# Seven PSUM banks given out by a plan of what is free first, and three small operations on the attention maxima moved

## The chip, the cores and the metric

The program runs on one core of one Trainium2 chip. The metric is the device time of one execution, in microseconds (us); lower is better. TensorE is called PE here (its weight loads PEld), VectorE is DVE, ScalarE is ACT, GpSimd is POOL, and SP is the engine that issues most DMAs.

## What is computed

The input is a batch of 4 sequences of 1024 tokens of width 128. Two transformer layers follow each other, each with 16 heads of width 8 and with attention and feed-forward side by side on the same normalised input:

```
xn = layernorm(x);  x = x + attention0(xn) + experts(xn)      # rotary, full softmax; top 2 of 8 experts, 128 -> 512 -> 128
xn = layernorm(x);  x = x + attention1(xn) + gated_fp4(xn)    # causal softmax; 4-bit rounded weights and activations, 128 -> 352 -> 128
```

Everything is fp32. The softmax is exact: each row's own maximum is subtracted before the exponential.

## The kernel before

**One order, written by a planner.** The class `Plan` (line 43) lays out 491 slots on the host, before the kernel is built. Every engine then walks the same list of slots and issues its own share of each, in order. The eight (layer, sequence) pairs are eight phases; a phase of layer 0 has 64 steps, one of layer 1 has 48, together 448.

**A slot.** A step of attention is one group of four heads against 128 keys and 512 queries. In its slot the function `products` makes, for each of four heads j, a matmul E (keys by queries, 50 rows contracted, 512 columns, in bf16) into one PSUM bank. ACT takes its exponential into `PR` (line 854), and PE multiplies that by the values into the bank `pO` in the slot after (eight fp32 matmuls). Beside each E stands a matmul M of scores the other way round (queries by keys, 48 rows) for a step twelve slots later (`AHEAD`). DVE takes the row maxima of M (line 1201, or line 1205 with the causal mask added) into `mparts`. E and M of the same j use different row halves of PE and are issued as a pair; PE waits for the banks of both before it issues either. So a slot takes eight banks for E and M.

**The maxima.** When a quarter of a phase's heads has its maxima for 512 queries ("combine", 64 times), DVE reduces `mparts` to the negated maximum `mneg` (128 x 16, line 1437), copies it to bf16 as its high part (line 1439), and writes the rest as the low part (line 1440), both into `msplit`. One slot later the event "mtr" turns `msplit` with one small matmul into a bank of the ring; DVE copies it to `mT` in bf16 (line 1473), and SP writes `mT` with four DMAs into two rows of `QX` (line 659). With these rows E comes out of the matmul with the maximum already subtracted.

**Everything else** ("xs", 551 events with the "mtr" ones) is spread by `Plan` over the slots: projections, transposes, the experts' tiles ("unit" and "y"), the fp4 feed-forward ("gu", "turn", "down"), and the ends of attention ("fin", "of", "fp"). PE does a slot's events after the second pair of products. Each event fills one bank, and either ACT or DVE empties it, as `ON_VECTOR` says. DVE's small steps (statistics, routing, scales) are planned into quarters of slots.

**The banks.** PSUM has eight banks: `pO`, and a ring of seven (`RING`). `number` (line 285) writes all 4135 fillings (E, M and events) in the order in which PE makes them, and filling number r uses bank r mod 7:

```
    def bank(self, kind, k):
        return self.at[kind][k] % RING
...
                def vacant(kind, k):
                    r = plan.at[kind][k] - RING
                    if r >= 0:
                        was, of = plan.ring[r]
```

so that PE always waits (in `vacant`) for the filling seven places back: on `s_ex` (an E read by ACT), `s_mr` (an M read by DVE) or `s_freed` (an event's bank).

Of the kernel before, what the change touches and what calls it, by code (L numbers as in the profile page):

```python
# [7 lines left out]
P = 128  # L8
HALF = 512
TH = HALF // P  # L10
DK = 8
G = 4
# [3 lines left out]
E, FC = 8, 4  # L16
# [3 lines left out]
PHASES = [(0, 0), (0, 1), (1, 0), (0, 2), (1, 1), (0, 3), (1, 2), (1, 3)]  # L20
# [7 lines left out]
RING = 7  # L28
# [4 lines left out]

ON_VECTOR = ("pj", "lg", "rt", "mtr", "fin", "gu", "down", "fp")
HEAVY = {"unit": 24, "y": 6, "turn": 11, "xT": 10, "v": 11, "cT": 10, "xqT": 10, "of": 10, "wT": 10,
         "pj": 11, "mtr": 8, "fin": 15, "gu": 8, "down": 5, "fp": 11, "lg": 5, "rt": 5}
SMALL = {"stats": 9, "means": 10, "norm": 12, "best": 5, "which": 8, "hits": 7, "comb": 12, "rem": 11, "wq": 15,
         "xq": 9, "hq": 6}  # L40


class Plan:
# [8 lines left out]
    def __init__(self):  # L52
        self.slots = []
        self.start = []
        self.place = {}
        at = LEAD + AHEAD
        for layer, b in PHASES:
            self.start.append(at)
            at += len(STEPS[layer])
        self.end = at  # L60
        for p, (layer, b) in enumerate(PHASES):
            i = self.start[p]
            for s in STEPS[layer]:
                self.slot(i)["step"] = (p,) + s
                self.slot(i + 1)["pv"] = (p,) + s
                g, qh, kt = s
                if g % 2 and kt == self.kts(p, qh) - 1:
                    self.slot(i + 1)["out"] = (p, g // 2, qh)
                    self.force(i + 2, ("fin", p, g // 2, qh))
                i += 1  # L70
            i = self.start[p] - AHEAD
            for q in QUADS[layer]:
                self.slot(i)["quad"] = (p,) + q
                g, qt, kh = q
                if qt % TH == TH - 1 and kh == (NH - 1 if layer == 0 else qt // TH):
                    self.slot(i)["combine"] = (p, g, qt // TH)
                    self.force(i + 1, ("mtr", p, g, qt // TH))
                    self.slot(i + 2)["sp"].append(("rows", p, g, qt // TH))
                i += 1
        self.prepare(0, 0)  # L80
        self.weights(12)
        for b in range(2):
            self.slot(LEAD + AHEAD - 2 + 24 * b)["sp"].append(("zero", b))
        for p, (layer, b) in enumerate(PHASES):
            if layer == 0:
                self.finish(p)
                if p:
                    self.tiles(p)
            else:
                self.finish(p)  # L90
            if p + 1 < len(PHASES):
                if PHASES[p + 1][0] == 0:
                    self.prepare(p + 1, self.start[p] - 20 if p else self.gated[p] + 2 * T + 2)
                    if p == 0:
                        self.tiles(p)
                else:
                    lead = max(self.start[p], self.done[PHASE_OF[0, PHASES[p + 1][1]]]) + 1
                    self.prepare(p + 1, lead)
        self.number()

    def kts(self, p, qh):
        return T if PHASES[p][0] == 0 else TH * (qh + 1)
# [44 lines left out]
    done = {}  # L147
# [137 lines left out]
    def number(self):  # L285
# [6 lines left out]
        for s in self.slots:  # L292
# [34 lines left out]
            for e in s["pool"]:  # L327
                if e[0] == "round" and e[-1] == POOL_STEPS - 2:
                    self.pools[e[1:-1]] = len(self.pools)

    def bank(self, kind, k):
        return self.at[kind][k] % RING


PLAN = Plan()
# [2 lines left out]
def two_layer_block(nc, x, wqa0, wqb0, wka0, wkb0, wv0, wo0, gate_w, gate_b, w1, b1, w2, b2wo,  # L338
# [3 lines left out]
    ALU, ACT, X = mybir.AluOpType, mybir.ActivationFunctionType, mybir.AxisListType.X  # L342
    plan = PLAN

    B, S, D = x.shape
# [19 lines left out]
    with ctx:  # L365
# [39 lines left out]
        stats = sb("stats", [P, T, 6])  # L405
# [13 lines left out]
        mparts = [sb(f"mparts{i}", [P, NH, G * TH, NH]) for i in range(2)]  # L419
        mneg = sb("mneg", [P, G * TH])  # L420
        msplit = sb("msplit", [P, 2 * G * TH], bf16)
        mT = sb("mT", [2 * G * TH, P], bf16)
# [22 lines left out]
        at = [sb(f"at{i}", [P, 2 * T], u32) for i in range(2)]  # L445
# [4 lines left out]
        cT = sb("cT", [E + 1, HALF])  # L450
# [5 lines left out]
        hq = sb("hq", [P, F1])  # L456
# [4 lines left out]
        xqT = sb("xqT", [P, S])  # L461
# [10 lines left out]
        s_x, s_freed = sem("s_x"), {"A": sem("s_xA"), "D": sem("s_xD")}  # L472
        s_pv, s_oT = sem("s_pv"), sem("s_oT")
        s_ng, s_row = sem("s_ng"), sem("s_row")
# [26 lines left out]
        xs = [nc.dram_tensor(f"rows_in{i}", (NT * P, D), f32, kind="Internal").ap() for i in range(2)]  # L501
# [19 lines left out]
        for o, w in ((0, wg), (o_up, wu)):  # L521
            for c in range(FC1):
                n = min(P, F1 - P * c)
# [23 lines left out]
        def copy(dst, src):  # L547
            return nc.scalar.activation(dst, src, ACT.Copy)  # L548
# [13 lines left out]
        def filled(e):  # L562
            return plan.xs[e] + 1
# [23 lines left out]
        with nc.Block() as block:  # L587
# [250 lines left out]
            def _(act):  # L838
# [19 lines left out]
                for i, s in enumerate(plan.slots):  # L858
# [5 lines left out]
                    if s["out"] is not None:  # L864
                        k = plan.outs[s["out"]]
# [7 lines left out]
                    for e in s["act"]:  # L873
                        _, p, q, h = e
                        n = plan.parts[p, q, h]
                        half = slice(HALF * h, HALF * h + HALF)
# [9 lines left out]
                    for e in s["xs"]:  # L886
                        if plan.by[e][0] == "A" or (e[0] == "gu" and e[3] == 0) or (e[0] == "pj" and e[4] == ""):
                            act.wait_ge(s_x, filled(e))
                        src = bank(e)
                        if e[0] == "xT":  # L890
                            _, p, h = e
                            layer, b = PHASES[p]
                            copy(flip[:, HALF * h:HALF * h + HALF], src[:, :]).then_inc(s_freed["A"], 1)
                        if e[0] == "pj" and e[4] == "":
                            _, p, q, h, _ = e
# [15 lines left out]
                        if e[0] == "y":  # L911
                            N, n = tile(*e[1:]), e[2]
                            if N >= 2 and n >= 0:
                                act.wait_ge(s_ys[N % 2], 16 * (N // 2))
                            c = slice(D if n < 0 else 0, D if n == NT - 1 else D + P)
                            copy(yx[N % 2][:, c], src[:, c]).then_inc(s_freed["A"], 1)
                        if e[0] == "unit":
# [6 lines left out]
                            for fc in range(FC):  # L924
                                ins = nc.scalar.activation(hid[N % 2][:, P * fc:P * fc + P], src[:, P * fc:P * fc + P],  # L925
                                                           ACT.Relu, bias=b1r[N % 2][:, fc:fc + 1])
# [3 lines left out]
                        if e[0] == "gu":  # L930
                            _, p, t, up = e
                            b = PHASES[p][1]
                            if up:
                                continue
                            if t or b:

                                was = (p, t - 1) if t else (PHASE_OF[1, b - 1], T - 1)
                                act.wait_ge(*freed(("gu",) + was + (0,)))
                            nc.scalar.activation(th[:, :], src[:, 0:F1], ACT.Tanh, scale=0.5).then_inc(s_th, 1)
                        if e[0] == "turn":  # L940
                            copy(hqT[:, 0:FC1 - 1, :], src[:, 0:(FC1 - 1) * P])
                            copy(hqT[0:FL, FC1 - 1, :], src[0:FL, (FC1 - 1) * P:FC1 * P]).then_inc(s_freed["A"], 1)
                        if e[0] == "of":
                            copy(ofT[:, :], src[:, :]).then_inc(s_freed["A"], 1)
                        if e[0] == "wT":
# [5 lines left out]
                    for e in s["late"]:  # L951
                        if e[0] == "mid":
                            _, p, q, h = e
                            n = plan.parts[p, q, h]
# [5 lines left out]
                        if e[0] == "abs":  # L960
                            n = plan.pools[e[1:]]
                            width = quantized(e[1:])[2]
# [4 lines left out]
            def _(pe):  # L967
                pe.wait_ge(s_wA, 16 * len(loads_a))

                def vacant(kind, k):  # L970

                    r = plan.at[kind][k] - RING
                    if r >= 0:
                        was, of = plan.ring[r]
                        if was == "E":
                            pe.wait_ge(s_ex, of + 1)
                        if was == "M":
                            pe.wait_ge(s_mr, of + 1)
                        if was == "X":
                            pe.wait_ge(*freed(of))  # L980
# [41 lines left out]
                for s in plan.slots:  # L1022
                    products(s, 0)
                    if s["pv"] is not None:
                        p, g, qh, kt = s["pv"]
                        n = plan.steps[s["pv"]]
# [8 lines left out]
                        first = kt == 0 and g % 2 == 0  # L1035
# [9 lines left out]
                    for e in s["xs"]:  # L1045
                        vacant("X", plan.xs[e])
                        dst = bank(e)
                        if e[0] == "xT":
                            _, p, h = e
                            for t in range(TH):  # L1050
                                pe.wait_ge(s_xn, T * p + TH * h + t + 1)
                                ins = turn(dst[:, P * t:P * t + P], xn[PHASES[p][0]][:, TH * h + t, :])
                        if e[0] == "pj":
                            _, p, q, h, part = e
                            layer, b = PHASES[p]
# [3 lines left out]
                            src = flip  # L1059
# [108 lines left out]
            def _(dve):  # L1168
# [9 lines left out]
                def count(ins):  # L1178
                    nonlocal counted
                    counted += 1  # L1180
                    ins.then_inc(s_dve, 1)

                def link(ins):
                    count(ins)
                    own()
# [243 lines left out]
                for s in plan.slots:  # L1429
# [4 lines left out]
                    if s["combine"] is not None:  # L1434
                        layer = PHASES[s["combine"][0]][0]
                        dve.wait_ge(s_mr, 4 * (plan.quads[s["quad"]] + 1))
                        link(v.tensor_reduce(mneg[:, :], mparts[layer][:, s["combine"][2], :, :], axis=X, op=ALU.max,
                                             negate=True))
                        link(v.tensor_copy(msplit[:, 0:G * TH], mneg[:, :]))
                        v.tensor_tensor(msplit[:, G * TH:2 * G * TH], mneg[:, :], msplit[:, 0:G * TH],  # L1440
                                        ALU.subtract).then_inc(s_ng, 1)
                    for e in s["small"][2]:
                        small_step(e)
                    for e in s["xs"]:
# [21 lines left out]
                                                  ALU.add)  # L1466
                        if e[0] == "rt":
                            ins = v.tensor_copy(before[:, :], src[:, 0:E * 2 * T + E])
                        if e[0] == "mtr":
                            k = plan.mtrs[e[1:]]  # L1470
                            if k:
                                dve.wait_ge(s_row, 64 * k)
                            ins = v.tensor_copy(mT[:, :], src[0:2 * G * TH, 0:P])
                        if e[0] == "fin":
                            _, p, g, qh = e
                            o4 = src[:, :].rearrange("p (q j w) -> p q j w", j=G, w=OW)
# [82 lines left out]
```

## Time and profile before

| | |
|---|---|
| median of 3 runs | 1598.43 us (1593.64 to 1598.57) |
| the profiled execution | 1606.22 us, of which its span is 1604.5 us |
| granted clock of PE, mean | 0.956 |
| instructions in the span | 34217 |

The profile gives one execution: busy time of each engine, what it waited for and who released it, the chain of work that ended last (followed back from the end to what released each piece), and each instruction's start. The median is used for the prediction; its steps are worked out on the profiled execution, whose own time is 7.8 us above that median.

### The profile page before, as it was taken

The numbers are of one execution on the slowest core, as the hardware profiler recorded it, in microseconds if no ns is written. First come the engines' busy times: TensorE is split into PE (matmuls) and PEld (weight loads), VectorE is DVE, ScalarE is ACT, GpSimd is POOL, SyncE is SP. The second block draws the span as 40 slices with busy tenths as digits, with TensorE's granted clock in tenths as the row PEclk, the third lists the DMA queues.
The fourth block names the chain that finished last, engine by engine and source line by source line (L and its number), as shares of the span: only waits on it lengthen the run. The fifth ranks groups of instructions, "written<-read, shape, count | busy, mean of one in ns | idle before, by whom it ended". The sixth has DMA issues, their size and how long they took to land.

```text
span 1604.5 us, 34217 instructions
## 1 busy us (share of the span) xinstructions
PE 1459.2 (91%) x10557; PEld 583.9 (36%) x10557; DVE 1338.2 (83%) x3450; ACT 1129.7 (70%) x2580; POOL 578.4 (36%) x531
## 2 busy tenths in 40 slices
PE   3978989999999899989999999989999988989986
PEld 1112344443333544432333444333433432323332
DVE  6999877789887698999888789889878779978991
ACT  2267678788787467777878767768878845765675
POOL 3002302103253456440242263660152464554443
PEclk8599999999999899999999999999999977989998
DMA  6403273333271452221451135123372100600000
GB/s 172 102 8 100 73 184 110 106 87 91 88 183 52 120 116 83 59 82 36 134 120 51 37 113 134 49 82 99 111 165 82 39 26 2 152 9 15 2 2 14
DMA packets 169833, 131.84 MB, mean 82 GB/s; under 512 B 31597, under 2 KB 143158, under 8 KB 169654
## 3 DMA queue, kind: packets, MB, share of 16 engines
q1 hardware_dynamic: 165562, 121.26, 28.5%
q0 software_dynamic: 4096, 8.40, 1.7%
q8 instruction: 91, 1.49, 0.4%
q14 instruction: 84, 0.69, 0.1%
HBM read 88.50 MB, written 40.50 MB: 80 GB/s over the span
## 4 chain that ended last, share of the span: by engine, by line
PE 58%; DVE 26%; issue 6%; ACT 5%; POOL 3%; DMA 1%; SPq 0%; another core or an unknown queue 0%; DVEq 0%; ACTq 0%; POOLq 0%
PE ring L542 38%; PE pO L542 17%; DVE mparts L1201 15%; PE ring L545 3%; ACT PR L854 3%; DVE junk L1205 2%; DVE xr L1381 1%; DVE stats L1251 1%; ACT hid L925 1%; DVE hs L1493 1%; DVE xr L1501 1%; DVE am L1414 1%; DMA b1r<-in_b 1%; ACT parts L548 0%; DVE hs L1489 0%
## 5 line engine op out<-in xcount | busy, mean ns | idle before, releaser
L854 ACT ACTIVATE PR<-ring 128x512 f32<-128x512 f32 (+3 forms) x1792 | 882.4, 557 | 344.8 <-PE ring L542 333.7
L1201 DVE TENSOR_REDUCE mparts<-ring 128x1 f32<-128x512 f32 x1280 | 808.5, 682 | 84.4 <-PE ring L542 77.1
L542 PE MATMUL ring<-QX,KX 50*128 50x512 bf16 (+3 forms) x1792 | 543.7, 366 | 77.2 <-DVE mparts L1201 35.5
L542 PE MATMUL ring<-KX,QX 48*128 48x512 bf16 (+3 forms) x1792 | 556.8, 374 | 14.2 <-DMA QX<-scratch 14.1
L542 PE MATMUL pO<-PR,VX 128*18 128x512 f32 (+3 forms) x3584 | 444.0, 568 | 6.5 <-ACT PR L854 5.2
L542 PEld LDWEIGHTS ring<-QX,KX 50*128 50x128 bf16 x1792 | 127.5, 94 | 609.0 <-ACT PR L854 220.3
L1205 DVE CUSTOM_DVE_ANT_0 junk<-ring,diag 128x384 bf16<-128x384 f32 (+3 forms) x512 | 228.8, 486 | 46.0 <-PE ring L542 41.2
L811 POOL TENSOR_SCALAR bq<-bq 128x352 f32<-128x352 f32 (+1 forms) x40 | 47.2, 1179 | 349.7 <-ACT bq L964 349.3
L784 POOL DMA_INDIRECT rows_in<-xn,at x64 | 63.7, 996 | 228.8 <-PE pO L542 144.8
L542 PEld LDWEIGHTS ring<-KX,QX 48*128 48x128 bf16 x1792 | 127.3, 94 | 33.6 <-DVE mparts L1201 17.9
L925 ACT ACTIVATE hid<-ring,b1r 128x128 f32<-128x128 f32 x368 | 105.0, 369 | 27.7 <-PE ring L542 26.2
L542 PE MATMUL ring<-yx,w1r 128*128 128x128 f32 x736 | 107.8, 291 | 7.7 <-DMA b1r<-in_b 4.8
L542 PEld LDWEIGHTS pO<-PR,VX 128*18 128x18 f32 x3584 | 60.6, 96 | 132.0 <-issue 88.0
L800 POOL DMA_INDIRECT ra<-rows_out,at x64 | 61.6, 963 | 125.4 <-PE pO L542 89.2
L542 PEld LDWEIGHTS ring<-yx,w1r 128*128 128x128 f32 x736 | 91.7, 196 | 34.3 <-DVE mparts L1201 23.3
L542 PE MATMUL ring<-w2r,hid 128*128 128x128 f32 x736 | 97.5, 275 | 0.0
L542 PEld LDWEIGHTS ring<-w2r,hid 128*128 128x128 f32 x736 | 93.2, 197 | 0.9 <-issue 0.5
L767 POOL TENSOR_TENSOR parts<-rb,parts 128x512 bf16<-128x512 f32 x30 | 35.0, 1166 | 115.3 <-ACT parts L548 115.3
L542 PE MATMUL ring<-identb,laterb 128*128 128x128 bf16 x512 | 75.2, 230 | 0.0
L825 POOL TENSOR_SCALAR yq<-yq 128x352 f32<-128x352 f32 (+1 forms) x40 | 60.3, 1508 | 3.3
L820 POOL TENSOR_TENSOR bq<-hq,bq 128x352 f32<-128x352 f32 x64 | 59.7, 933 | 4.6
L548 ACT ACTIVATE yx<-ring 128x256 f32<-128x256 f32 (+1 forms) x96 | 36.0, 375 | 35.2 <-PE ring L542 33.8
(165 smaller groups left out, 1349.8 us busy)
## 6 DMA issues: line engine op xcount, KB each, us to landing
w1r<-in_w SPq DMA_DIRECT2D x92, 256.0 KB
w2r<-in_w SPq DMA_DIRECT2D x92, 256.0 KB
scratch<-parts SPq DMA_DIRECT2D x48, 256.0 KB, 3.3
scratch<-parts SPq DMA_DIRECT2D x96, 128.0 KB, 2.3
KX<-scratch SPq DMA_DIRECT2D x64, 192.0 KB, 4.4
QX<-scratch SPq DMA_DIRECT2D x128, 96.0 KB, 5.0
xg<-rows_in SPq DMA_DIRECT2D x92, 64.0 KB
rows_out<-yx SPq DMA_DIRECT2D x92, 64.0 KB
```

Of the source, the lines that this page charges most:

```text
L542: return nc.tensor.matmul(dst, lhsT, rhs, start=start, stop=stop, **kw)
L545: return nc.tensor.transpose(dst, src, ident[0:src.shape[0], 0:src.shape[0]])
L548: return nc.scalar.activation(dst, src, ACT.Copy)
L784: nc.gpsimd.indirect_dma_start(xs[b % 2], bass.IndirectOffsetOnAxis(at[b % 2][:, c:c + 1], 0), xn[0][:, c % T, :], None).then_inc(s_sc[b], 16)
L800: nc.gpsimd.indirect_dma_start(yg[:, D * t:D * t + D], None, ys[b % 2], bass.IndirectOffsetOnAxis(at[b % 2][:, c:c + 1], 0)).then_inc(s_yg ...
L811: ins = nc.gpsimd.tensor_scalar(b_, b_, 1.0, None, ALU.max)
L820: ins = nc.gpsimd.tensor_tensor(b_, dst, b_, ALU.subtract)
L825: ins = nc.gpsimd.tensor_scalar(y, y, SHIFT, SHIFT, ALU.add, ALU.subtract)
L854: nc.scalar.activation(PR[:, n % 2, HALF * j + off:HALF * j + HALF], ring[plan.bank("E", k)][:, off:HALF], ACT.Exp, scale=SCALE).then_inc( ...
L925: ins = nc.scalar.activation(hid[N % 2][:, P * fc:P * fc + P], src[:, P * fc:P * fc + P], ACT.Relu, bias=b1r[N % 2][:, fc:fc + 1])
L1201: v.tensor_reduce(dst, src[:, 0:w], axis=X, op=ALU.max).then_inc(s_mr, 1)
L1205: v.tensor_tensor_reduce(out=junk[k % 2][:, 0:w], in0=src[:, 0:w], in1=diag[:, HALF - w:HALF], scale=1.0, scalar=NEG, op0=ALU.add, op1=ALU ...
```

## The change

Three things are changed. `banks`, a new function of `Plan`, walks the slots with a list of work for PE, ACT and DVE, with constant costs for each piece and a constant lag between engines, and gives each filling the bank that by these costs is free first; it remembers whose bank that was (`was`), and `vacant` waits for that filling. The number of banks, PE's order and each engine's order of the events stay. Second, the copy of the turned maxima to `mT` goes from DVE to ACT, where it is done among the slot's events, after the slot's exponentials. Third, the high part of the maxima is no longer a copy of `mneg`, but a second reduction straight from `mparts` with bf16 output, which does not wait for the first. Because DVE no longer copies `mT`, the combine now waits in so many words for the "mtr" matmul before it (`s_x`).

```
-ON_VECTOR = ("pj", "lg", "rt", "mtr", "fin", "gu", "down", "fp")
+ON_VECTOR = ("pj", "lg", "rt", "fin", "gu", "down", "fp")
...
+ON_TENSOR = {"unit": 13, "y": 14, "turn": 8, "xT": 11, "v": 13, "cT": 11, "xqT": 11, "of": 11, "wT": 10, "pj": 17,
+             "mtr": 4.6, "fin": 11, "gu": 12.5, "down": 9, "fp": 18, "lg": 13, "rt": 8}
+
+EMPTIES = {"unit": 16.5, "y": 6.2, "turn": 7, "xT": 8, "v": 9, "cT": 8, "xqT": 8, "of": 8, "wT": 8, "pj": 10, "mtr": 4,
+           "fin": 12.5, "gu": 8.7, "down": 5, "fp": 11.5, "lg": 4, "rt": 5}
+STEP = {"stats": 6.6, "means": 4.4, "norm": 8.4, "best": 2.8, "which": 4.5, "hits": 4.5, "comb": 8.8, "rem": 10, "wq": 18}
+SIDE, PV, MASK, LAG = 3.7, 13.5, 4, 4.5
...
         self.number()
+        self.banks()
...
+    def banks(self):
+        work = {"P": [], "A": [], "D": []}
+        step_cost = lambda e: (8.5, 2.2, 5.2, 7.5)[e[-1]] if e[0] in ("xq", "hq") else STEP.get(e[0], 3)
+        for s in self.slots:
...
+                        work["P"].append((SIDE * max(ew, mw) / 4 if c is pair[0] else 0, (), c, [] if masked else [c]))
...
+                    work["P"].append((2 + PV * pw / 4, [("ex", 4 * n + j) for j in range(4)], None, [("pv", n)]))
...
+                        work["A"].append((1.2 + 1.65 * ew, [("E", k)] + [("pv", k // 4 - 2)] * (k >= 8), None, [("ex", k)]))
...
+                        work["D"].append(((2 if PHASES[quad[0]][0] == 0 else 1.3) + (2 if PHASES[quad[0]][0] == 0 else 2.2) * mw, [("M", k)], None, [("mx", k)]))
...
+            for e in s["xs"]:
+                work["P"].append((ON_TENSOR[e[0]], (), ("X", self.xs[e]), [("X", e)]))
...
+                work[self.by[e][0]].append((EMPTIES[e[0]], [("first" if first else "X", e)], None, [("done", e)]))
...
+        held = [None] * RING
+        self.bank_of, self.was = {}, {}
+
+        def advance(who):
+            while place[who] < len(work[who]):
+                cost, needs, takes, gives = work[who][place[who]]
+                if any(t not in time for t in needs):
+                    return
+                clock[who] = max([clock[who]] + [time[t] + LAG for t in needs])
+                if takes is not None:
+                    free = lambda b: -1 if held[b] is None else time.get(held[b][1], math.inf)
+                    b = min(range(RING), key=free)
+                    clock[who] = max(clock[who], free(b) + LAG)
+                    self.bank_of[takes], self.was[takes] = b, held[b] and held[b][0]
...
     def bank(self, kind, k):
-        return self.at[kind][k] % RING
+        return self.bank_of[kind, k]
...
+                        if e[0] == "mtr":
+                            k = plan.mtrs[e[1:]]
+                            if k:
+                                act.wait_ge(s_row, 64 * k)
+                            copy(mT[:, :], src[0:2 * G * TH, 0:P]).then_inc(s_freed["A"], 1)
...
-                    r = plan.at[kind][k] - RING
-                    if r >= 0:
-                        was, of = plan.ring[r]
+                    if plan.was[kind, k] is not None:
+                        was, of = plan.was[kind, k]
...
-                        link(v.tensor_reduce(mneg[:, :], mparts[layer][:, s["combine"][2], :, :], axis=X, op=ALU.max,
-                                             negate=True))
-                        link(v.tensor_copy(msplit[:, 0:G * TH], mneg[:, :]))
+                        n = plan.combines[s["combine"]]
+                        if n:
+                            dve.wait_ge(s_x, filled(("mtr",) + list(plan.combines)[n - 1]))
+                        parts_ = mparts[layer][:, s["combine"][2], :, :]
+                        count(v.tensor_reduce(mneg[:, :], parts_, axis=X, op=ALU.max, negate=True))
+                        link(v.tensor_reduce(msplit[:, 0:G * TH], parts_, axis=X, op=ALU.max, negate=True))
                         v.tensor_tensor(msplit[:, G * TH:2 * G * TH], mneg[:, :], msplit[:, 0:G * TH],
                                         ALU.subtract).then_inc(s_ng, 1)
...
-                        if e[0] == "mtr":
-                            k = plan.mtrs[e[1:]]
-                            if k:
-                                dve.wait_ge(s_row, 64 * k)
-                            ins = v.tensor_copy(mT[:, :], src[0:2 * G * TH, 0:P])
```

## Rows read from the trace of the kernel before

**Rows 1.** The page, section 1: busy us, share of the span, instructions.

```profile
PE 1459.2 (91%) x10557; PEld 583.9 (36%) x10557; DVE 1338.2 (83%) x3450; ACT 1129.7 (70%) x2580; POOL 578.4 (36%) x531
```

**Rows 2.** The page, section 4: chain that ended last, by engine.

```profile
PE 58%; DVE 26%; issue 6%; ACT 5%; POOL 3%; DMA 1%; SPq 0%; another core or an unknown queue 0%; DVEq 0%; ACTq 0%; POOLq 0%
```

**Rows 3.** Waits of PE: in total, times, longest.

```profile
PE ring L542 <- DVE mparts L1201: 45.3, 97, 2.1
PE ring L542 <- ACT PR L854: 23.0, 49, 2.1
PE ring L542 <- DMA QX<-scratch: 14.1, 1, 14.1
PE ring L545 <- DVE xn L1268: 11.0, 1, 11.0
PE ring L542 <- DVE mparts L1205: 6.6, 10, 2.5
PE ring L545 <- DVE mparts L1201: 5.5, 11, 1.1
```

**Rows 4.** Timeline around 429 us: start us, us, work, [idle before <-releaser].

```profile
427.98 1.11 ACT L854 ACTIVATE PR<-ring 128x512 f32<-128x512 f32 x2
...
428.86 0.68 DVE L1426 SCALAR_TENSOR_TENSOR yq<-xn,ri 128x512 f32<-128x512 f32 x1
...
429.00 0.39 PE L542 MATMUL ring<-QX,KX 50*128 50x512 bf16 x1
429.00 0.39 PE L542 MATMUL ring<-KX,QX 48*128 48x512 bf16 x1
429.46 1.88 DVE L1201 TENSOR_REDUCE mparts<-ring 128x1 f32<-128x512 f32 x3
...
430.20 0.33 PE L545 MATMUL ring<-ident,xg 128*128 128x128 f32 x1 [0.81 <-DVE mparts L1201]
```

**Rows 5.** Timeline from 115 us, a step without other work.

```profile
114.71 7.70 DVE L1201 TENSOR_REDUCE mparts<-ring 128x1 f32<-128x512 f32 x12
...
117.09 0.59 PE L542 MATMUL ring<-QX,KX 50*128 50x512 bf16 x2
...
117.31 0.38 PE L542 MATMUL ring<-KX,QX 48*128 48x512 bf16 x1
...
118.08 0.37 PE L542 MATMUL ring<-QX,KX 50*128 50x512 bf16 x1 [0.40 <-DVE mparts L1201]
...
118.48 1.05 PE L542 MATMUL pO<-PR,VX 128*18 128x512 f32 x8
...
120.69 0.37 PE L542 MATMUL ring<-QX,KX 50*128 50x512 bf16 x1 [0.40 <-DVE mparts L1201]
```

**Rows 6.** Timeline of PE: first and last of the 98 bank waits.

```profile
67.00 0.58 PE L542 MATMUL ring<-QX,KX 50*128 50x512 bf16 x1 [0.58 <-DVE mparts L1201]
...
1561.09 0.37 PE L542 MATMUL ring<-QX,KX 50*128 50x512 bf16 x1 [0.20 <-DVE mparts L1201]
```

**Rows 7.** Groups by line: the DVE instructions that the change touches.

```profile
L1473 DVE CAST mT<-ring 32x128 bf16<-32x128 f32 x64 | 17.2, 269 | 1.2 <-PE ring L542 1.1
...
L1439 DVE CAST msplit<-mneg 128x16 bf16<-128x16 f32 x64 | 15.1, 236 | 2.2
...
L1440 DVE TENSOR_TENSOR msplit<-mneg,msplit 128x16 bf16<-128x16 f32 x64 | 13.0, 203 | 2.2
...
L1437 DVE TENSOR_REDUCE mneg<-mparts 128x16 f32<-128x32 f32 x64 | 11.9, 186 | 2.2
```

**Rows 8.** Groups by line: ACT work nearest to the moved copy.

```profile
L854 ACT ACTIVATE PR<-ring 128x128 f32<-128x128 f32 x128 | 28.6, 276 | 29.6 <-PE ring L542 28.5 <-PE pO L542 0.6
...
L548 ACT ACTIVATE hqT<-ring 96x128 f32<-96x128 f32 x32 | 9.0, 281 | 0.0
```

**Rows 9.** Groups by line: the maxima on DVE, exponentials on ACT.

```profile
L1201 DVE TENSOR_REDUCE mparts<-ring 128x1 f32<-128x512 f32 x1280 | 808.5, 682 | 84.4 <-PE ring L542 77.1 <-issue 1.1
L854 ACT ACTIVATE PR<-ring 128x512 f32<-128x512 f32 x1408 | 756.0, 604 | 237.6 <-PE ring L542 230.6 <-PE pO L542 2.1 <-issue 2.1
```

**Rows 10.** Waits of ACT.

```profile
ACT PR L854 <- PE ring L542: 333.7, 440, 34.4
```

More of the change, by code:

```diff
@@ L329, in number @@
                     self.pools[e[1:-1]] = len(self.pools)
+    def banks(self):
+        work = {"P": [], "A": [], "D": []}
+        step_cost = lambda e: (8.5, 2.2, 5.2, 7.5)[e[-1]] if e[0] in ("xq", "hq") else STEP.get(e[0], 3)
+        for s in self.slots:
+            step, quad = s["step"], s["quad"]
+            width = lambda key, which: 4 if key is None or PHASES[key[0]][0] == 0 else (
+                max(1, 4 - max(0, key[3] - TH * key[2])) if which == "E" else min(4, key[2] + 1 - TH * key[3]))
+            ew, mw = width(step, "E"), width(quad, "M")
+            for half in range(2):
+                js = (2 * half, 2 * half + 1)
+                for j in js:
+                    pair = [(kind, 4 * n[key] + j) for kind, key, n in
+                            (("E", step, self.steps), ("M", quad, self.quads)) if key is not None]
+                    for c in pair:
+                        masked = c[0] == "E" and step in self.masks
+                        work["P"].append((SIDE * max(ew, mw) / 4 if c is pair[0] else 0, (), c, [] if masked else [c]))
+                if step in self.masks:
+                    work["P"].append((MASK, (), None, [("E", 4 * self.steps[step] + j) for j in js]))
+                if half == 0 and s["pv"] is not None:
+                    n = self.steps[s["pv"]]
+                    pw = width(s["pv"], "E")
+                    work["P"].append((2 + PV * pw / 4, [("ex", 4 * n + j) for j in range(4)], None, [("pv", n)]))
+                if step is not None:
+                    for j in js:
+                        k = 4 * self.steps[step] + j
+                        work["A"].append((1.2 + 1.65 * ew, [("E", k)] + [("pv", k // 4 - 2)] * (k >= 8), None, [("ex", k)]))
+                if quad is not None:
+                    for j in js:
+                        k = 4 * self.quads[quad] + j
+                        work["D"].append(((2 if PHASES[quad[0]][0] == 0 else 1.3) + (2 if PHASES[quad[0]][0] == 0 else 2.2) * mw, [("M", k)], None, [("mx", k)]))
+                if half == 0:
+                    if s["out"] is not None:
+                        work["A"].append((8, [("pv", self.steps[s["pv"]])], None, ()))
+                    work["A"] += [(9, (), None, ()) for e in s["act"]]
+                    work["D"] += [(step_cost(e), (), None, ()) for q in s["small"][:2] for e in q]
+            if s["combine"] is not None:
+                work["D"].append((10, (), None, ()))
+            work["D"] += [(step_cost(e), (), None, ()) for e in s["small"][2]]
+            for e in s["xs"]:
+                work["P"].append((ON_TENSOR[e[0]], (), ("X", self.xs[e]), [("X", e)]))
+                first = (e[0] == "gu" and not e[3]) or (e[0] == "pj" and e[4] == "")
+                if first:
+                    work["A"].append((8 if e[0] == "pj" else 6.2, [("X", e)], None, [("first", e)]))
+                work[self.by[e][0]].append((EMPTIES[e[0]], [("first" if first else "X", e)], None, [("done", e)]))
+            work["A"] += [(2 if e[0] == "gates" else 7.5, (), None, ()) for e in s["late"]]
+            work["D"] += [(step_cost(e), (), None, ()) for e in s["small"][3]]
+        freeing = {"E": "ex", "M": "mx"}
+        time, at, clock, place = {}, [], {"P": 0, "A": 0, "D": 0}, {"P": 0, "A": 0, "D": 0}
+        held = [None] * RING
[11 more added lines that the diff above has]
+                    self.bank_of[takes], self.was[takes] = b, held[b] and held[b][0]
+                    held[b] = (gives[0], ("done", gives[0][1])) if takes[0] == "X" else (
+                        takes, (freeing[takes[0]], takes[1]))
+                clock[who] += cost
+                for g in gives:
+                    time[g] = clock[who]
+                place[who] += 1
+                if who == "P" and (place[who] == len(work[who]) or work[who][place[who]][0]):
+                    return
+        while place["P"] < len(work["P"]):
+            advance("P")
+            advance("A")
+            advance("D")
```

## The prediction, made before the changed kernel was run

> **What bounds the kernel now.** I read the page's busy times first: PE is busy 91% of the span, DVE 83%, ACT 70% [rows 1]. That alone would say that PE is full. But PE's ends are modelled and a stalled row of matmuls counts as busy, so I went on to the chain that ended last: it runs through PE for 58%, through DVE for 26%, through ACT for 5% [rows 2]. No engine is the bound by itself. PE and DVE pass the chain to and fro, and the question is how.
>
> The waits of PE tell [rows 3]. Two large single waits belong to the start (14.1 us for the first operands, 11.0 us for the first normalisation), and the change does not touch them. The repeated ones are for a bank: DVE's maxima let go of it late (45.3 us in 97 waits, 6.6 in 10 and 5.5 in 11), or ACT's exponentials (23.0 us in 49): 80.4 us in which PE visibly stood still.
>
> Is it a bank that is missing, or only the next in the ring? Two places in the timeline answer differently.
>
> Around 429 us [rows 4] an event "y" wants a bank. The two products before it start at 429.00, so PE could go on at about 429.3. The ring gives it the bank seven fillings back, an M whose reduction is the first of the three that begin at 429.46, after DVE's other work from 428.86 on; it starts at 430.20. Two exponentials had ended at 427.98 + 1.11 = 429.09, and the bank of the second of them was empty by then. PE lost 0.9 us to the order alone.
>
> From 115 us on, in slots without events [rows 5], it is different. DVE makes twelve maxima without a pause in 7.70 us, 0.64 us each, and PE starts the same pair every 2.61 us (118.08, 120.69) with a wait of 0.40 in front. Four maxima of 0.64 fill the 2.61: DVE is the bound, all banks are rightly held, and no other order of banks helps.
>
> **The change part by part.**
>
> *Banks.* I laid the plan's order of all 4135 fillings beside the trace: for each, when PE could have started it (start of PE's instruction before, plus the usual distance of such a pair, such as 0.22 us from one pair of products to the next [rows 5]), when it did start, and when each of the seven banks had been emptied. PE's starts are 211 us late in all because the bank seven back was emptied less than 0.4 us before; in 106 us of that, enough banks for what was to come were already empty. Most of it lies where the chain does not pass, and only shortens a wait that is there for something else. So I kept the hand-overs from DVE or ACT to PE in the chain. There are 123; 98 are waits for a bank, the first at 67.00 and the last at 1561.09 us [rows 6], together 64.6 us late, and in 31.1 us of these another bank was empty. This is the term: **-31 us**. Both ends of it: nothing, if the plan's times are so poor that its choice is no better than the next in turn, and -65 us, if a looser order lets PE run ahead and DVE never starves after it.
>
> *DVE.* The copy of mT goes: 17.2 us. The cast to bf16, 15.1 us, becomes a reduction of 32 elements such as the one that makes mneg, 11.9 us, so 3.2 us less. It no longer waits for that one, which saves the gap of 2.2 us. Sum 22.6 us of DVE [rows 7]. Of DVE's busy time 26/83 = 31% is on the chain [rows 1, 2], so **-7 us**. The added wait of the combine, for the "mtr" matmul before it, costs nothing: that lies several slots back, and DVE waited for the same matmul before (1.2 us in all, [rows 7]). Behind it on DVE stand the next maxima, and for them PE, so if "mtr" ever were late, PE would wait too; nothing in the rows shows it.
>
> A word on the swap. By the medians the two are nearly equal: the cast's mean of 236 ns is pulled up by a few long ones. The row of the reduction says 186 ns, and I take that. The Trainium skill (VectorE: DVE Perf Modes, The perf-mode tier table) says that a reduction has only the 1x mode while an fp32 copy in SBUF has 2x, which speaks against this swap. By its cycle table the 32 elements would take 25 ns more than the copy, an estimate of 1.6 us more over 64 instead of 3.2 less.
>
> *ACT.* It gets 64 copies of 32 x 128 out of PSUM. The nearest rows are an exponential of the same width, 276 ns, and a copy of 96 x 128, 281 ns [rows 8]: 64 x 0.28 = 17.9 us. ACT waits 333.7 us for PE's products in 440 waits [rows 10], which covers it. Without that cover the share of ACT's busy time that lies on the chain (5 of 70, [rows 1, 2]) prices it: **+1 us**. Ends: 0 and +18. The copy stands behind the slot's exponentials and before the other events, so a late "mtr" would hold up the next emptying and the next exponentials. PE makes "mtr" just after the last pair of the slot, however, and ACT is busy with that pair's exponentials for 1.1 us [rows 4]. SP's four DMAs for the rows now wait for ACT's copy; SP's order is the same, and the rows are wanted slots later.
>
> *What the plan gets wrong.* Its costs are constants; the real engines are held by DMAs, POOL and a clock that is not always granted in full. Where it names a bank that is in fact held, PE waits although the ring's bank might be free. The nearest price is one reduction, 0.68 us, or one exponential, 0.60 [rows 9]. I estimate nine such waits on the chain: **+6 us**. Ends: 0, and the whole 31.
>
> *Sum.* -31 - 7 + 1 + 6 = -31 us against the profiled execution's own 1606.2 us, so 1575. That execution stands 7.8 us above the median of 1598.4; the same step from the median gives **1567 us**, 1.9% less. A measurement of this kernel can tell some 0.3%, 5 us, from no change.
>
> **The rivals.**
>
> *Looser than I think (chance 0.14).* Elasticity feeds on itself: with seven banks in turn one slow M stops PE after six more fillings, three of them M; given out freely, ACT's banks come back at once and DVE may fall behind by about five. The 106 us with an empty bank would then count for most of their value. Against it: every second wait had no empty bank. The sum would be -75 - 7 + 7 = -75: 1523 us.
>
> *DVE takes over (0.20).* Slots as in [rows 5] are the rule: PE gets ahead and then waits for the next maximum with all seven banks full. For it: the chain already has DVE for 26%. Against it: DVE stands idle 266 us of the span [rows 1]. Then a third of the banks' term is left, and DVE's relief counts: -10 - 7 + 7 = -10: 1588 us. That the change does not do what it says comes to the same: if the planned order mostly names the ring's own bank, only DVE's 22.6 us are touched, 1592 us.
>
> *Misplanned banks (0.14), slower.* The place is each slot where DVE's small steps or a wait for POOL or a DMA make the M banks come free later than the E banks, the opposite of the constants. The plan has no means of noticing, and what it gets wrong by one bank costs a whole reduction of 0.68 us. The gain of 31 + 7 us is gone at 38/0.68 = 56 such waits on the chain, one in eight of the 448 slots; at 85, one in five, the time is 20 us above: 1618 us. Against it: the costs look measured. If the plan's units are a fifteenth of a us, 10 for a maximum is 0.67 and 7.8 for an exponential is 0.52, near [rows 9]. A page's rule points the same way: the Trainium skill (Perfetto Trace Analysis, Matmuls) wants independent groups to rotate through the banks, which is what the ring does and the plan gives up. The rows say that rotation has a price [rows 4].
>
> **How the numbers follow.** The forecast has 0.52 and its own range is 1550 to 1582. The range for 8 in 10 goes to 1538 on one side, which leaves out most of the loose case, and to 1602 on the other, which takes in the case of DVE and leaves out most of the misplanned one. Faster by over 0.3%, below 1593.6: 0.52 + 0.14 + 0.12 (three fifths of DVE's case), 0.78. Within 0.3%: the other 0.08 of that case and 0.02 of the misplanned one, 0.10. Slower: the rest of the misplanned one, 0.12.
>
> **What the profile after would show.** Right: PE's waits for mparts and PR (80.4 us before) fall by a third or more; PE rises towards 93% busy; DVE's busy time falls by about 20 us to 1318, and ACT's rises by 18 to 1148; the chain's PE share rises. The place of an "y" event shows no wait while ACT's bank is empty. Wrong: PE's bank waits stay near 80 us with fewer but longer ones, a releaser named that frees its bank after another was empty (misplanned); or they fall while DVE's waits for PE stay and the span does not move (DVE's work in slots is the bound). A wait of ACT for "mtr" of more than a few us would put the copy's move in doubt.

## The result: faster by 0.9%, less than half of what was forecast

The changed kernel takes 1585.96 us, median of 10 runs; the kernel before, run beside it, 1597.87. One of the ten, of 3093 us, was disturbed; without it the median is 1584.42, and the ratio, which leaves it out too, is 0.9915 (95% interval 0.9897 to 0.9934), 13.6 us less. The forecast was 1567, 31 us less, with a range from 1538 to 1602. The time lies in the range and on the forecast side, but the gain is less than half of the one that was named. The profiled execution took 1583.88 us.

The page of the changed kernel, sections 1 and 4:

```profile
PE 1445.1 (91%) x10557; PEld 578.0 (37%) x10557; DVE 1318.5 (83%) x3386; ACT 1138.8 (72%) x2644; POOL 577.9 (37%) x531
...
PE 66%; DVE 11%; issue 6%; ACT 6%; POOL 5%; SPq 3%; DMA 2%; DVEq 0%; ACTq 0%; POOLq 0%
```

DVE is relieved by 19.7 us, as forecast (1318), and its share of the chain falls from 26% to 11% while PE's rises from 58% to 66%. PE's busy share stays at 91% (93 was named), and ACT's busy time rises by 9 us, from 1129.7 to 1138.8, where 18 were named. What PE waits for, in the same kernel (us in total, times, longest):

```profile
PE ring L632 <- ACT PR L944: 38.2, 77, 1.1
PE ring L632 <- DVE mparts L1295: 20.9, 52, 1.2
...
PE ring L632 <- DVE mparts L1299: 7.4, 12, 1.4
```

Here line 1295 is line 1201 of the kernel before, 1299 is 1205, and 944 is 854. Against [rows 3] the waits for DVE's maxima fall from 57 to 28 us, and those for ACT's exponentials rise from 23 to 38. Together they fall by a sixth, where a third was named as the sign of a right forecast.

The moved copy, and the high part straight from the maxima (minimum/median/maximum in ns):

```profile
L638 ACT ACTIVATE mT<-ring x64: 249/254/267, 57.8 to 1545.0; 32x128 bf16<-32x128 f32 x64
...
L1537 DVE TENSOR_REDUCE msplit<-mparts x64: 174/176/178, 56.9 to 1542.3; 128x16 bf16<-128x32 f32 x64
```

The copy costs ACT 64 x 0.254 = 16.3 us, near the 17.9 named. The prediction held that a wait of ACT for "mtr" of more than a few us would put this move in doubt. There is one, of 27.3 us, but it stands before the very first "mtr" (the copy at 57.8 us), before ACT has any exponential to take, and at slot 40 both kernels are level (below). Only one other such wait is in the trace; the two together are 27.7 us.

**Where the gain goes.** PE does the same matmuls in the same order in both kernels, so each slot can be given a start in either trace: its first matmul. Up to slot 40 the two are level (71.7 against 71.9 us). At slot 52 the change is 14.6 us *behind* (129.3 against 114.7), and at the last slot 22.4 us ahead. So the whole loss stands in twelve slots, nearly all of it in the first seven (slots 40 to 46, 14.6 us from their start to their end), and the 437 after slot 52 gain 37 us in this pair of profiles. The windows of these twelve slots, the changed kernel and then the kernel before (us; busy of PE, PEld, DVE, ACT, POOL with counts; granted clock, DMA share, GB/s):

```profile
71.70:129.30 57.60, 46.33 (x225) 12.39 (x225) 42.52 (x108) 28.65 (x56) 2.06 (x2) 0.64 0.01 3
```

```profile
71.90:114.70 42.80, 34.86 (x229) 9.53 (x225) 41.59 (x109) 26.52 (x53) 1.33 (x2) 0.90 0.02 4
```

DVE has the same 42 us of work in both. Before, it fills the stretch; in the change it stands idle for 15 us. PE's granted clock is 0.64 on average instead of 0.90: in the change it stays at 1.2 GHz until 113.7 us, where in the kernel before it first rises to 2.4 GHz at 73.5 us and stays there from 90.6 on. For the same matmuls PE is busy for 46.3 us instead of 34.9. A piece of the timeline of the changed kernel shows how:

```profile
97.01 0.60 PE L632 MATMUL ring<-QX,KX 50*128 50x512 bf16 x1 [0.75 <-ACT PR L944]
...
97.65 0.60 ACT L944 ACTIVATE PR<-ring 128x512 f32<-128x512 f32 x1 [0.70 <-PE ring L632]
97.69 0.69 DVE L1295 TENSOR_REDUCE mparts<-ring 128x1 f32<-128x512 f32 x1 [0.66 <-PE ring L632]
...
98.31 0.60 PE L632 MATMUL ring<-QX,KX 50*128 50x512 bf16 x1 [0.68 <-ACT PR L944]
...
98.98 0.69 DVE L1295 TENSOR_REDUCE mparts<-ring 128x1 f32<-128x512 f32 x1 [0.60 <-PE ring L632]
99.01 0.60 ACT L944 ACTIVATE PR<-ring 128x512 f32<-128x512 f32 x1 [0.66 <-PE ring L632]
...
99.66 0.60 PE L632 MATMUL ring<-QX,KX 50*128 50x512 bf16 x1 [0.74 <-ACT PR L944]
```

One product, its exponential, the next product: 1.3 us a round, with nothing beside it but DVE's reduction, which waits for PE as well. PE waits for the bank of the product that it made just before. The plan says why. Of the 4128 fillings that take over a bank, 98 take one filled only 2 to 4 fillings before, and 29 of these stand in slots 40 to 50, 22 of them in slots 40 to 46. By the plan's costs (15 of its units to a us) DVE is far behind there: the first M of slot 42 is emptied 7.6 us after it is filled. So the plan counts most banks as held by M, and sends E round on the few left. In the trace that M is emptied after 2.9 us, while ACT and PE pass E's banks to each other. In part that is the stall's own doing: without it the same M is emptied after 4.1 us (the kernel before) or 5.7 (e5 below), so DVE does fall behind there, but by less than planned.

### The profile page after: what moved, and what is told of

It is laid out like the page before. It is cut to its first block, busy times and chain, and to the rows that moved or that the text cites. A ratio compares the mean times of both kernels' runs of the same rounds, so it can differ in the third digit from the quotient of the medians.

```text
span 1582.1 us, 34276 instructions
## 1 busy us (share of the span) xinstructions
PE 1445.1 (91%) x10557; PEld 578.0 (37%) x10557; DVE 1318.5 (83%) x3386; ACT 1138.8 (72%) x2644; POOL 577.9 (37%) x531
## 4 chain that ended last, share of the span: by engine, by line
PE 66%; DVE 11%; issue 6%; ACT 6%; POOL 5%; SPq 3%; DMA 2%; DVEq 0%; ACTq 0%; POOLq 0%
PE ring L632 42%; PE pO L632 20%; DVE mparts L1295 6%; ACT PR L944 5%; PE ring L635 4%; SPq L718 1%; DVE junk L1299 1%; POOL bq L910 1%; ACT hid L1015 1%; POOL yq L915 1%; POOL yq L912 1%; POOL bq L901 1%; POOL rows_in L874 1%; DVE xr L1475 0%; DMA b1r<-in_b 0%
## 5 line engine op out<-in xcount | busy, mean ns | idle before, releaser
L632 PE MATMUL ring<-QX,KX 50*128 50x512 bf16 (+3 forms) x1792 | 536.7, 366 | 75.0 <-ACT PR L944 34.5
L915 POOL TENSOR_SCALAR yq<-yq 128x352 f32<-128x352 f32 (+1 forms) x40 | 60.2, 1506 | 3.3
L912 POOL TENSOR_SCALAR yq<-yq 128x352 f32<-128x352 f32 (+1 forms) x40 | 60.2, 1506 | 0.1
```

What stands on the lines that cost most here:

```text
L632: return nc.tensor.matmul(dst, lhsT, rhs, start=start, stop=stop, **kw)
L912: ins = nc.gpsimd.tensor_scalar(y, y, -1.0, 1.0, ALU.max, ALU.min)
L915: ins = nc.gpsimd.tensor_scalar(y, y, SHIFT, SHIFT, ALU.add, ALU.subtract)
```

## The experiments

All of them were run beside the kernel before on the same chip; "ratio" is to that kernel. The chip was not the same for all experiments, so two of them are compared by their ratios. A slot's time is that of its first matmul, as above.

**e1, the ring's banks with the two moves.** The order of banks undone, the rest kept:

```diff
+        turn_of = iter(range(len(self.ring)))
...
-                    b = min(range(RING), key=free)
+                    b = next(turn_of) % RING
```

> The ring's order of banks (filling number modulo seven), with the mT copy on ScalarE and the high part straight from mparts. Theory A (the plan of banks gave the gain after slot 60 and lost 15 us in slots 40 to 50): only DVE's relief is left, 3 to 8 us faster than before, 1590 to 1595, and slots 40 to 50 take 36 us as before, not 51. Theory B (the moved copy on ScalarE causes the loss in slots 40 to 50): the 15 us are lost here too, 1600 to 1610.

Measured: 1603.55 us, ratio 1.0022 (1.0001 to 1.0042). Slots 40 to 52 take 42.6 us, so the moves have no part in that loss and theory B falls. But DVE's relief is worth nothing here: the kernel is 3.5 us slower than before, barely clear of noise, and not 3 to 8 faster as expected.

**e2, the planned banks alone.** "mtr" back in `ON_VECTOR`, the copy and the cast on DVE as before.

> The planned banks, with the mT copy and the cast on VectorE as before. Theory A: the loss of 15 us in slots 40 to 50 is here, and the gain after them nearly whole: 1588 to 1594. Theory B: no loss in slots 40 to 50, so faster than the change itself, about 1575. Theory C (the moves carry the gain, the banks nothing): 1598 or slower.

Measured: 1596.83 us, ratio 0.9996 (0.9973 to 1.0019), slots 40 to 52 in 50.3 us. The loss is there without the moves, if smaller: 7.5 us more than the 42.8 of the kernel before. The time fits neither expectation: A was 1588 to 1594, C 1598 or slower. A had the place right, but the gain after it is not nearly whole, 19 us in this profile against the 37 of the change. Neither part alone makes the kernel faster; together they do.

**e3, banks in turn at the start.** The changed kernel, with one line replaced (`turn_of` as in e1):

```diff
-                    b = min(range(RING), key=free)
+                    r = next(turn_of)
+                    b = r % RING if r < self.at["E"][4 * 14] else min(range(RING), key=free)
```

> The whole change, but up to the 14th step (slot 52) banks go in turn, and by the plan only after that. Theory A: slots 40 to 50 take about 36 us again and the rest keeps its gain: 1568 to 1574, 12 to 15 us faster than the change. Theory D (the loss there is the granted clock's own, 1.2 GHz instead of 2.4, and has nothing to do with the banks): 1584 as the change, with slots 40 to 50 as long as in the change.

Measured: 1574.82 us, ratio 0.9846 (0.9799 to 0.9893). Slots 40 to 52 take 42.6 us, and the time is 11 us below the change's (0.9846 against 0.9915). That is theory A's account, at the slow end of its 12 to 15 us.

**e4, no bank of the last four fillings.**

```diff
+        last = [None] * 4
...
-                    b = min(range(RING), key=free)
+                    b = min((b for b in range(RING) if b not in last), key=free)
+                    last = last[1:] + [b]
```

> The whole change, but the plan may not give a filling the bank of one of the four fillings before it. Theory A (short reuse is what costs, since PE then waits for the filling it has just made): most of the 15 us in slots 40 to 50 comes back, and some more where the change reuses a bank after 2 to 4 fillings later on (98 of 4114 fillings in all): 1568 to 1578. If short reuse is harmless: 1584, as the change.

Measured: 1574.74 us, ratio 0.9839 (0.9798 to 0.9881), slots 40 to 52 in 44.9 us. A plan from first to last that may not reuse a bank at once is as good as one that starts late. (The count of fillings in the expectation should be 4128.)

**e5, PE priced double in slots below 52.**

```diff
+            cold = 2 if i < 52 else 1
...
-                        work["P"].append((SIDE * max(ew, mw) / 4 if c is pair[0] else 0, (), c, [] if masked else [c]))
+                        work["P"].append((cold * SIDE * max(ew, mw) / 4 if c is pair[0] else 0, (), c, [] if masked else [c]))
```

and the same for the values' matmuls and for the events.

> The whole change, planned from the start, but the plan prices TensorE's work at twice the cost in slots below 52, where its granted clock was 1.2 GHz for most of the time. Theory A (the loss is a plan made for a VectorE that lags and a TensorE at 2.4 GHz, which is not what runs there): the slots 40 to 52 take 43 us instead of 58, and the whole 1570 to 1580. If the loss is not the plan's prices: 1584 and 58 us as in the change.

Measured: 1572.54 us, ratio 0.9825 (0.9798 to 0.9853). Its slots 40 to 52:

```profile
70.90:113.30 42.40, 35.23 (x229) 9.65 (x225) 41.25 (x108) 26.94 (x55) 1.35 (x2) 0.87 0.02 4
```

The same instructions, the same planner, one price changed for 52 slots: the 15 us are back. In that plan one filling of slots 40 to 50 reuses a bank within four. So the short reuse comes from the price of PE against that of DVE. That the doubled price is the true one is not shown. PE's granted clock in the kernel before is 0.51 from 25 to 72 us, up to slot 40, but 0.83 from there to 96.4 us; and e5's plan gives slots 40 to 52 57 us, where its trace takes 42, while the change's plan gives them 46, near the 43 of the kernel before. What e3, e4 and e5 share is that the short reuse in these slots is gone.

**e9, the same mistake made on purpose where the clock is full.** On top of e3, DVE's maxima priced double in slots 200 to 210; 37 of their fillings reuse a bank after 3 or 4.

> The run with banks in turn up to the 14th step, but the plan prices VectorE's maxima at twice their cost in slots 200 to 210, where the granted clock was 2.4 GHz, so that it reuses banks after 3 or 4 fillings there (43 times). Theory A: slots 200 to 210 take 8 to 14 us more than the 32.5 of the correct price. Theory D (short reuse costs only at 1.2 GHz): less than 3 us more.

Measured: 1587.28 us, ratio 0.9924 (0.9893 to 0.9955), 12 us above e3's. (The profiled execution, 1594.14 us, was the slowest of five.) Slots 200 to 210, with the wrong price and (e3) with the right one:

```profile
625.20:672.10 46.90, 34.92 (x246) 14.45 (x246) 31.52 (x64) 26.66 (x64) 14.41 (x14) 0.95 0.15 45
```

```profile
626.00:658.50 32.50, 31.23 (x246) 13.47 (x246) 29.59 (x62) 24.91 (x64) 13.72 (x13) 1.00 0.18 48
```

The same work, 14.4 us longer, just above theory A's 8 to 14. The granted clock is full from 625.2 to 667.1 us, which is 42 of these 47 us. Theory D falls: short reuse costs at 2.4 GHz as well. At the start the slow clock goes with the stall, and the change's order of banks prolonged it, since with e3's and e5's orders the clock first rises at 74.0 and 72.1 us, as before; how much of the 15 us it added by itself was not measured apart. (The 43 of the expectation were counted with the slots around.)

**e8 and e10, banks by the trace.** e8 has e3's start; after it a list of digits in the source gives each filling the bank that was empty first in e3's own trace. e10 is the same from e8's trace.

```diff
-                    b = min(range(RING), key=free)
+                    b = int(BANKS[next(turn_of)])
```

> Moves and ring start as in the run with banks in turn up to the 14th step; after it the banks come from a list that gives each filling the bank that was empty first in that run's own trace. Theory G (what the constants misjudge elsewhere costs as well): 5 to 15 us faster than 1575. Theory H (beyond the start the plan is as good as the true times): 1572 to 1578.

> The list of banks made once more, now from the trace of the run with measured banks. If the measured order converges: 1560 to 1566, the same within 0.3%. If each list only suits the trace that it was made from: 5 to 15 us slower than 1564.

Measured: e8 1564.25 us, ratio 0.9767 (0.9738 to 0.9796); e10 1559.97 us, 0.9784 (0.9761 to 0.9808). Theory G: the constants cost another 13 us over the rest of the kernel (0.9846 against 0.9767), and the second list brings nothing more. I counted the late starts of PE once more as in the prediction, from slot 52 on: 97 us of them had another bank empty in the kernel before, 59 in the change, 24 in e8. No view of the profile prints this count; its fall is to be read and not its exact size. The waits of PE in e8:

```profile
PE ring L676 <- DVE mparts L1339: 28.9, 66, 2.1
PE ring L676 <- ACT PR L988: 20.1, 53, 0.8
```

The waits for ACT, which the plan had raised to 38 us, are at the ring's level again. e8 and e10 beat both kernels, by 2.3% and 2.2% against the kernel before.

**e7 and e13, the planned banks without the moves.** e7 is e3 with the copy and the cast on DVE; e13 is e7 with the high part straight.

> Banks in turn up to the 14th step, planned after it, with the mT copy and the cast on VectorE as before the change. Theory E (with planned banks VectorE's relief of 22 us counts, with the ring it does not): 10 to 15 us slower than the same start with the moves (1575), so 1585 to 1590. Theory F (the moves are worth nothing in either): 1573 to 1578.

> Banks in turn up to the 14th step and planned after it, with only the high part straight and the mT copy on VectorE. If the 14 us between the runs with and without the two moves belong to the mT copy: 1584 to 1589. If they belong to the high part: 1573 to 1578.

Measured: e7 1588.89 us, ratio 0.9944 (0.9919 to 0.9968); e13 1588.79 us, 0.9940 (0.9922 to 0.9957). With planned banks the moves are worth 0.9944 - 0.9846 = 1.0%, 16 us, and the move of the copy of mT is what counts: e13 and e3 differ only by it and the combine's wait that goes with it. e7 also qualifies e2: without the bad start the planned banks are 0.6% faster than the ring by themselves.

**e11 and e12, each move alone in the ring.**

> Banks in the ring's order, only the mT copy moved to ScalarE, the combine as before. Theory I (in the ring, the later release of the mtr bank and ScalarE's extra 16 us cancel what VectorE saves): 1598 to 1604, as slow as both moves together. Theory J (the copy's move is good in the ring as well, and the straight high part is what costs): 1590 to 1595.

> Banks in the ring's order, only the high part straight from mparts, the mT copy on VectorE as before. 64 x 0.08 us less of VectorE at most: 1594 to 1600 by either theory but J, by which it is 1600 to 1606.

Measured: e11 1605.01 us, ratio 1.0047 (1.003 to 1.0065); e12 1595.01 us, 0.9976 (0.9956 to 0.9996). The high part straight from the maxima is worth some 4 us in the ring, barely clear of noise, and nothing with planned banks (e13 against e7). The copy on ACT, the same move that brings most of 1.0% with planned banks, costs 0.5% in the ring.

**e14, e15, e16, second profiles** of the kernel before, of e11 and of the change.

> The kernel before, unchanged, for a second profile. If the place at slots 167 to 171 (32 us in the first profile, 26 with the mT copy on ScalarE) is a matter of that copy, it takes 32 us again; if it varies from one execution to the next, some other time.

> The ring's order with only the mT copy on ScalarE, a second profile. The first was 6 us below the profile of the kernel before while the medians say 7 us above. If one place costs the difference, it shows against the second profile of the kernel before; if it is spread, the differences by slot drift upwards evenly.

> The changed kernel, a second profile. Slots 40 to 52 take 57 to 58 us again if their loss is fixed by the plan, and less in some executions if it hangs on the clock.

Measured, one execution each: 1602.46, 1615.61 and 1587.72 us. The change takes 57.7 us for slots 40 to 52 again (57.6 the first time): the loss is fixed by the plan. Slots 167 to 172 take 32.1 and 30.5 us in the kernel before and 32.1 in e7, all with the copy on DVE; 24.3 and 25.9 in e11's two profiles, 24.3 in e3 and in both of the change, with the copy on ACT. In all profiles that were taken this place takes 30.3 to 32.2 us with the copy on DVE and 23.0 to 25.9 with it on ACT, so it holds some 5 to 8 us of the move's gain, in the ring as well. In e7 and in e3 it looks so:

```profile
518.70:550.80 32.10, 28.11 (x180) 15.27 (x181) 16.70 (x53) 14.28 (x39) 17.48 (x16) 0.84 0.33 100
```

```profile
511.20:535.50 24.30, 23.12 (x177) 12.26 (x177) 16.83 (x52) 13.62 (x38) 13.75 (x13) 1.00 0.32 96
```

DVE's work differs by 0.1 us, the span by 8: projections go there through ACT, POOL and DVE in turn, and the longer stretch has a granted clock of 0.84 instead of 1.00. In the ring the gain is given back elsewhere: e15 loses 4.5, 4.0, 3.8, 3.5 and 3.3 us against e14 in slots 179, 281, 285, 401 and 398. e11's first profile has part of that. Nothing that was run says why these slots suffer from the copy on ACT only while the banks go in turn; this stays open.

## Why the prediction was wrong

**The reading of the bound held.** PE and DVE pass the chain to and fro through banks that are held in the wrong order, and an order by what is free first is worth much: with both moves in place the banks planned from slot 52 on bring e1's 1.0022 down to e3's 0.9846, 28 us, where the term was -31. Lists made from the trace bring another 13 us.

**The term that failed is the plan's mistakes, +6 us.** It was priced as nine waits of one reduction on the chain. The runs show 11 to 14 us in slots 40 to 52 alone (the change against e3 and e5, 0.9915 against 0.9846 and 0.9825) and 13 us more in the rest (e8 against e3): some 24 us in all by e3. The size of one mistake was about right: the waits in the timeline above are 0.68 to 0.75 us, one exponential or reduction was named [rows 9]. What was wrong is that I spread them as single errors. A plan with a wrong ratio of two engines' prices is wrong all through a stretch: it closes E's banks into a short round, so that up to four pairs a slot each wait for one exponential. The rival "misplanned banks" had the sign reversed: DVE's banks came free earlier than planned, not later. It also had the price of a slot too small: a misplanned slot cost 2 us in slots 40 to 46 and 1.4 in e9, not one wait of 0.68.

The banks' own term was undersized, which hid part of this. The mistakes are counted against the order made from a trace, and that order is worth 0.0255, 41 us (e1 against e8), not 31. Banks and mistakes together come to 41 - 24 = 17 us of gain, where 31 - 6 = 25 were forecast. That the 28 us of e3 lie near the -31 is luck: they are the 41 less the 13 that its plan still loses.

**DVE's relief, -7 us, and ACT's load, +1 us,** failed as well. They were sized by shares of the chain. DVE's busy time came out as forecast, the effect did not: +3.5 us in the ring (e1), -16 us with planned banks (e3 against e7). It is no sum of independent terms, and a share of the chain could not show that. The weighed rule on the swap: the Trainium skill (VectorE: DVE Perf Modes, The perf-mode tier table) gives a reduction only the 1x mode. The reduction took 176 ns at the median, the cast that it replaced 175 to 236 [rows 7], and the kernel with that swap alone is 0.2% faster (e12), so the rule's estimated loss of 1.6 us did not show; a time alone could hardly have shown so little, the two medians of 176 and 175 ns do.

**On rotation.** The Trainium skill (Perfetto Trace Analysis, Matmuls) wants independent groups to rotate through the banks. Measured, both sides have a point: strict rotation costs 2.5% here (e1 against e8), and giving it up by a wrong price costs more in ten slots (14.4 us, e9) than the right one gains in a hundred (some 9, if e8's 41 us are spread evenly over its slots). e4, which only forbids the last four, keeps most of both.

The sum with measured terms: +3.5 (moves in the ring), -28 (banks from slot 52 on), +11 (slots 40 to 52, by e3) gives -13.6 us. It comes out by construction, since the three are the steps from the kernel before over e1 and e3 to the change; it says where the 31 went and tests nothing.

## What to carry to other kernels

Where buffers are handed out ahead of time by modelled costs, compare the plan's own times with the trace for every stretch, and look first for buffers that are reused right after they were filled: a floor on the distance of reuse cost nothing here and took out the worst mistake. When the order can be fixed in the source, make it from a trace of the kernel rather than from constants. And test small moves together with the change of order that they come with: here neither part as written was faster alone (e1, e2), and together they were.

## What the runs showed of the hardware

A stall and the granted clock went together at the start: where PE waited in short rounds its granted clock was 0.64, against 0.90 for the same work without the waits, and PE's busy time for that work 46.3 us against 34.9. In e9 the waits came at a full clock; it fell to 1.2 GHz at 667.1 us, after 42 us of them, and the ten slots were 14.4 us longer all the same. One place of the program held up to 8 us, half a per cent, on a copy of 0.25 us moved to another engine (slots 167 to 172, e7 against e3).
